# Scores and maxima of a causal attention as float32r products in row halves, the other products cut in row halves, and the causal mask added by a product

## The reference

```python
x = x + 0.5 * ffn(layernorm(x))
x = x + attention(layernorm(x))
x = x + 0.5 * ffn(layernorm(x))

# ffn: x_prev is x shifted by one row
r = sigmoid((mu_r * x + (1 - mu_r) * x_prev) @ W_r.T)
k = (mu_k * x + (1 - mu_k) * x_prev) @ W_k.T
out = r * (square(relu(k)) @ W_v.T)

# attention, per head, after a rotation of q and k by position
att = softmax(where(causal, q @ k.T / sqrt(16), -1e9))
out = (att @ v) @ W_proj + b_proj
```

## Time and profile before

| | us |
|---|---|
| median of 3 runs | 3111.19 |
| lowest and highest | 3110.26, 3119.8 |
| the profiled execution | 3112.07 |
| its span in the trace | 3110.3 |
| TensorE busy | 2962.3 (95%) |
| VectorE busy | 2475.0 (80%) |
| ScalarE busy | 2159.2 (69%) |
| GpSimd busy | 1566.6 (50%) |

### The profile page before, as it was taken

One profiled execution on the slowest core, in us unless ns is written; L12 is line 12 of the kernel. 1 busy time (PEld: TensorE's weight loads), 2 busy tenths in 40 slices (PEclk: granted clock), 3 DMA queues, 4 the chain that ended last, 5 costly groups with the idle time before them and its releaser, 6 DMA issues.

```text
span 3110.3 us, 56224 instructions
## 1 busy us (share of the span) xinstructions
PE 2962.3 (95%) x18245; PEld 1665.9 (54%) x18245; DVE 2475.0 (80%) x7302; ACT 2159.2 (69%) x4802; POOL 1566.6 (50%) x2190
## 2 busy tenths in 40 slices
PE   6899999999999999999999999999999999999997
PEld 4444555555555555555555555555555555555444
DVE  3888888888888888888888887888888888887872
ACT  4477777777777777777777777777767777777664
POOL 5455555555455455555555455454555555454323
PEclk9899999999999999999999999999999999999999
DMA  3443343343434352342443333343442532433421
GB/s 99 79 84 65 64 100 66 83 90 72 86 77 88 69 97 67 76 99 60 91 87 68 88 77 84 80 85 76 79 93 59 98 81 67 93 76 71 83 60 39
DMA packets 202585, 245.49 MB, mean 79 GB/s; under 512 B 68405, under 2 KB 104245, under 8 KB 202293
## 3 DMA queue, kind: packets, MB, share of 16 engines
q1 hardware_dynamic: 202293, 241.90, 37.5%
HBM read 53.48 MB, written 51.38 MB: 34 GB/s over the span
## 4 chain that ended last, share of the span: by engine, by line
PE 66%; DVE 12%; ACT 8%; POOL 6%; issue 6%; DMA 1%; SPq 1%; POOLq 0%; DVEq 0%; ACTq 0%
PE ps_y L735 14%; PE ps_s L704 12%; PE ps_m L714 11%; PE ps_d L794 7%; PE ps_d L788 6%; PE ps_d L791 5%; PE ps_d L800 5%; ACT pt_sb L830 4%; DVE ps_m L943 3%; PE ps_d L781 3%; PE ps_d L742 2%; DVE mx_sb L946 2%; PE ps_d L804 2%; POOL pt_sb L1075 2%; DVE dif_sb L974 2%
## 5 line engine op out<-in xcount | busy, mean ns | idle before, releaser
L830 ACT ACTIVATE pt_sb<-ps_s 128x512 f32<-128x512 f32 (+1 forms) x3039 | 1451.6, 495 | 816.9 <-PE ps_s L704 806.7
L943 DVE CUSTOM_DVE_ANT_0 ps_m<-ps_m,mask_sb 128x128 f32<-128x128 f32 (+3 forms) x2048 | 990.3, 498 | 370.7 <-PE ps_m L714 355.9
L704 PE MATMUL ps_s<-qr_sb,kr_sb 99*128 99x512 bf16 (+1 forms) x3039 | 994.5, 329 | 50.4 <-ACT pt_sb L830 39.3
L714 PE MATMUL ps_m<-kr_sb,qr_sb 96*128 96x512 bf16 (+3 forms) x3072 | 1000.1, 329 | 37.9 <-DVE mx_sb L943 27.7
L946 DVE TENSOR_REDUCE mx_sb<-ps_m 128x1 f32<-128x512 f32 x1024 | 697.9, 682 | 105.7 <-PE ps_m L714 97.3
L1075 POOL TENSOR_SCALAR_AFFINE_SELECT pt_sb<-pt_sb 128x512 f32<-128x512 f32 x512 | 331.4, 647 | 833.8 <-ACT pt_sb L830 833.3
L735 PE MATMUL ps_y<-pt_sb,v_sb 128*32 128x512 f32 (+3 forms) x6144 | 589.9, 494 | 3.6 <-POOL pt_sb L1075 2.7
L704 PEld LDWEIGHTS ps_s<-qr_sb,kr_sb 99*128 99x128 bf16 x3039 | 291.8, 96 | 510.0 <-issue 229.7
L714 PEld LDWEIGHTS ps_m<-kr_sb,qr_sb 96*128 96x128 bf16 x3072 | 302.0, 98 | 319.2 <-DVE mx_sb L943 71.1
L800 PE MATMUL ps_d<-axn_sb,wqk_sb 128*128 128x256 f32 x1024 | 305.3, 396 | 3.9 <-ACT axn_sb L872 3.9
L735 PEld LDWEIGHTS ps_y<-pt_sb,v_sb 128*32 128x32 f32 x6144 | 154.6, 109 | 285.9 <-issue 258.3
(11 more groups left out here) (96 smaller groups left out, 3465.5 us busy)
## 6 DMA issues: line engine op xcount, KB each, us to landing
kr_sb<-part_sb SPq DMA_DIRECT2D x378, 128.0 KB, 4.4
qr_sb<-part_sb SPq DMA_DIRECT2D x378, 128.0 KB, 4.7
y_way<-yt_sb SPq DMA_DIRECT2D x128, 256.0 KB, 2.7
sw_sb<-qb_sb SPq DMA_DIRECT2D x496, 64.0 KB, 2.0
x_sb<-x SPq DMA_DIRECT2D x64, 256.0 KB, 2.8
yn_sb<-y_way SPq DMA_DIRECT2D x64, 256.0 KB
den_sb<-r_way SPq DMA_DIRECT2D x64, 256.0 KB
out<-x_sb SPq DMA_DIRECT2D x64, 256.0 KB, 2.2
```

Of the source, the lines that this page charges most:

```text
L704: eng.matmul(score_bank(slot)[:, 0:width], kr_sb[0:KR + NP, n % RS, j, kb * P:(kb + 1) * P], qr_sb[0:KR + NP, n % RS, j, q0:q0 + width], s ...
L714: eng.matmul(ps_m[:, u % NM, 0:width], qr_sb[0:KR, n % RS, j, i * P:(i + 1) * P], kr_sb[0:KR, n % RS, j, piece * QC:piece * QC + width], s ...
L830: eng.activation(pt_sb[:, buffer, j, column:column + width], score_bank(slot)[:, 0:width], ACT.Exp, scale=SCALE).then_inc(exped, 1)
L943: eng.tensor_tensor_reduce(ps_m[:, u % NM, 0:width], ps_m[:, u % NM, 0:width], mask_sb[:, m0:m0 + width], 1.0, -3e38, ALU.add, ALU.max, be ...
```

## The change

- Scores and maxima become float32r products. q and k are cut into two parts, three pairs of parts make 48 rows (`KR`), and two rows take the maximum. Two of a group's four heads lie in rows 0 to 63 of `qr_sb` and `kr_sb`, two in rows 64 to 127. In each slot the score is in one half of the rows and the maximum in the other. Products less than 256 columns wide are widened to 256.
- The mask is added to a diagonal maximum by a second, bfloat16 product of 128 columns into the same bank (`later_sb`, `pairs_sb`), and VectorE takes all maxima with the plain reduction. There are two banks `ps_m` in place of three, and three `ps_d` in place of two.
- Each planned product is made in two passes over half the rows, "lanes": first with rows 0 to 63, later with rows 64 to 127 added into the same bank. A slot holds one matmul of each lane, lane 1 of one product and lane 0 of the next (`place_pe`). Outside slots -53 to 3071 they stay whole. Transposes are halved too, lane 0 ahead of the score and lane 1 behind the maximum.
- `r_rest` and `r_mid` are gone, and the buffers `qb_sb` and `sw_sb`: the bias goes straight into `part_sb`, so `r_b0` and not `r_hi` now waits for the DMAs that read the batch before. `rows` has three steps of four DMAs in place of six of two. `m_fin` makes two parts; its maxima end 17 slots ahead (`LEAD`). The maxima keep the order of alternating widths (row block 7, 0, 6, 1, ...), now all four heads of one piece in a row.

```diff
-TERMS_Q = (0, 0, 0, 1, 1, 2)
-TERMS_K = (0, 1, 2, 0, 1, 0)
+TERMS_Q = (0, 0, 1)
+TERMS_K = (0, 1, 0)
...
-NP = 3
+NP = 2
+HALF = P // 2
 VW = HS + 1
 VPAD = 32 - VW
-NEG = -1e30
+BIG, TINY = 2.0 ** 55, 2.0 ** -16
 SCALE = HS ** -0.5
 
-NS, NM, ND = 2, 3, 2
+NS, NM, ND = 2, 2, 3
...
-MAX_ORDER = [i for k in range(TT // 2) for i in (TT - 1 - k, k)]
-UNITS = [(i, j, piece) for i in MAX_ORDER for j in range(G) for piece in range(i // KQ + 1)]
-NU = len(UNITS)
-LEAD = 13
+PIECES = [(i, piece) for k in range(TT // 2) for i in (TT - 1 - k, k) for piece in range(i // KQ + 1)]
+LEAD = 17
+NU = GSLOTS
+UNITS = [(PIECES[u // G][0], (u - LEAD) % G ^ 1, PIECES[u // G][1]) for u in range(NU)]
...
+PATIENCE = 3
...
-                    s("ACT", "r_b0", i, 0.36, t, ("r_QK", i, 1), ("r_low", i - 2 if i >= NCH + 2 else -1, 1))
+                    s("ACT", "r_b0", i, 0.36, t, ("r_QK", i, 1), (f"rows{NT - 1}", NG * (b - 1) + 2 * pair + 1, 7))
...
-                    s("ACT", "r_hi", i, 0.53, t, ("r_add", i, 3), (f"rows{NT - 1}", NG * (b - 1) + 2 * pair + 1, 7))
-                    s("POOL", "r_rest", i, 1.2, t, ("r_hi", i, 2))
-                    s("ACT", "r_mid", i, 0.53, t, ("r_rest", i, 3))
-                    s("POOL", "r_low", i, 1.2, t, ("r_mid", i, 2))
+                    s("ACT", "r_hi", i, 0.53, t, ("r_add", i, 3))
+                    s("POOL", "r_low", i, 1.2, t, ("r_hi", i, 2))
...
+    def place_pe(self, chains, slot, mine):
+
+        whole = slot < HALF_MAX or slot >= self.nb * BSLOTS
...
+        if free and self.entire is None and self.lanes[0] is None and not (whole and self.lanes[1]):
+            key = self.pick("PE", chains, slot, None)
+            if key:
+                self.hold(key, free[0])
+                self.slots[key[0] + "+", key[1]] = slot
+                if whole:
+                    self.entire = key, 0
+                else:
+                    self.lanes[0], self.idle = (key, 0), 0
+                    self.divide(key)
...
+        if self.lanes[0] is None and (self.lanes[1] is None or self.idle < PATIENCE and not whole):
+            self.idle += 1
+            return 0, 0
+        done = 0
+        for lane in (1, 0):
+            if self.lanes[lane]:
+                key, u = self.lanes[lane]
+                units = self.steps[key][1]
+                if u < units:
+                    mine.append((*key, u, lane))
+                self.lanes[lane] = key, u + 1
+                if lane == 1 and u + 1 == units:
+                    self.lanes[1] = None
+                    self.slots[key] = slot
+                    done = 1
+                if lane == 0 and u + 1 >= units and self.lanes[1] is None:
+                    self.lanes = [None, (key, 0)]
...
-        part_sb = sb("part_sb", [P, NP, 2, 2, T], BF16)
-        v_sb = sb("v_sb", [P, 2, TT, H * VW + VPAD])
-        qr_sb = sb("qr_sb", [P, RS, G, T], BF16)
-        kr_sb = sb("kr_sb", [P, RS, G, T], BF16)
+        part_sb = sb("part_sb", [P, NP, 2, 2, T])
+        v_sb = sb("v_sb", [P, 2, VPAD + TT * H * VW])
+        qr_sb = sb("qr_sb", [P, RS, G // 2, T], F32R)
+        kr_sb = sb("kr_sb", [P, RS, G // 2, T], F32R)
...
+                            for h in range(2):
+                                r = HALF * h + t * HS
+                                eng.dma_start(dst[r:r + HS, ring, :, cols].bitcast(F32),
+                                              part_sb[base + h:base + 64:2, part, m, n, cols]).then_inc(rows_in[ring], 16)
...
+                rows, more = slice(HALF * (j % 2), HALF * (j % 2) + KR + NP), max(0, CH - width)
+                eng.matmul(score_bank(slot)[:, 0:width + more], kr_sb[rows, n % RS, j // 2, kb * P:(kb + 1) * P],
+                           qr_sb[rows, n % RS, j // 2, q0 - more:q0 + width], start=True, stop=True).then_inc(scored, 1)
...
+                rows, wide = slice(HALF * (j % 2), HALF * (j % 2) + KR), max(CH, width)
+                product = eng.matmul(ps_m[:, u % NM, 0:wide], qr_sb[rows, n % RS, j // 2, i * P:(i + 1) * P],
+                                     kr_sb[rows, n % RS, j // 2, piece * QC:piece * QC + wide], start=True, stop=not diagonal)
+                if diagonal:
+                    half = slice(HALF * (j % 2), HALF * (j % 2) + HALF)
+                    pe.wait_ge(masks_in, 32)
+                    product = eng.matmul(ps_m[:, u % NM, width - P:width], later_sb[half, :], pairs_sb[half, :], start=False, stop=True)
+                product.then_inc(max_made, 1)
...
-            def dense(name, i, u):
+            def dense(name, i, u, lane):
+
                 d = plan.bank[name, i]
-                if u == 0:
+                if u == 0 and not lane:
                     pe.wait_ge(taken[d], plan.nth[name, i])
+                if u == 0 and lane == 1:
+                    pe.wait_ge(half_made[d], plan.split[name, i])
                 ps = ps_d[:, d, :]
                 h, cc = divmod(u, CC)
-                cols, rows = slice(h * P, (h + 1) * P), halves(h)
+                cols, out_cols = slice(h * P, (h + 1) * P), halves(h)
+                k = slice(0, P) if lane is None else slice(HALF * lane, HALF * lane + HALF)
...
+                if u == units - 1:
+                    mm.then_inc(half_made[d] if lane == 0 else made[d], 1)
...
-                m0 = QC + P - width
-                dve.wait_ge(set_pool, N_SET_POOL)
                 dve.wait_ge(max_made, u + 1)
-                best = mx_sb[:, n % 2, piece, j * TT + i:j * TT + i + 1]
-                if diagonal:
-                    eng.tensor_tensor_reduce(ps_m[:, u % NM, 0:width], ps_m[:, u % NM, 0:width], mask_sb[:, m0:m0 + width],
-                                             1.0, -3e38, ALU.add, ALU.max, best).then_inc(max_taken, 1)
-                else:
-                    eng.tensor_reduce(best, ps_m[:, u % NM, 0:width], mybir.AxisListType.X, ALU.max).then_inc(max_taken, 1)
+                m = j % 2 * NH + j // 2 * TT + i
+                eng.tensor_reduce(mx_sb[:, n % 2, piece, m:m + 1], ps_m[:, u % NM, 0:width], mybir.AxisListType.X,
+                                  ALU.max).then_inc(max_taken, 1)
...
-                elif name == "r_rest":
+                elif name == "r_low":
                     pool.wait_ge(r_high, i + 1)
-                    eng.tensor_tensor(biased_of(i), biased_of(i), parts_of(i, 0), ALU.subtract).then_inc(r_rest, 1)
-                elif name == "r_low":
-                    pool.wait_ge(r_mid, i + 1)
-                    eng.tensor_tensor(parts_of(i, 2), biased_of(i), parts_of(i, 1), ALU.subtract).then_inc(r_low, 1)
+                    eng.tensor_tensor(rounded(parts_of(i, 1)), biased_of(i), parts_of(i, 0), ALU.subtract).then_inc(r_low, 1)
```

428 lines of the change are left out of this document (208 added, 220 removed).

## The result

The changed kernel takes 3464.72 us (median of 4, 3460.28 to 3469.01) beside 3113.94 us for the kernel before on the same chip: a ratio of 1.1124, 95% interval 1.11 to 1.1149. It is 11% slower, and slower than the whole range of the forecast. Its profiled execution has a span of 3462.0 us, against 3110.3.

A forecast was written before the change was run, and what follows sets the result against it. TensorE was taken as the bound, 175.7 us of a 187.5 us batch; it falls to 152.1, other engines and waits make it 162 + 13 = 175.0, 12.5 fewer a batch; 3112.1 - 192 = 2920 us, range 2830 to 2990.

The forecast's parts named there:

- TensorE is the bound before, with short waits on banks: Kernel before: TensorE needs 175.7 of a batch's 187.5 us, and 11.8 are left as waits.
- Halves side by side, and float32r at the pace of bfloat16: Assumptions for TensorE: both row halves run at once; scores and maxima fall from 63.6 to 33.4 us a batch.
- in line: Rival: planned passes start strictly in list order, costing 17.2 us a batch; 3020 us in all; chance 0.13.
- slow float32r: Rival: float32r scores and maxima stream at a float32 pass's pace, 0.43 us for 512 columns; 3222 us; chance 0.08.
- not together: Rival: the array's row halves don't run together, so their times add up; 4258 us; chance 0.07.
- 0.22 for a pass of 512: TensorE price of a score or maximum of 512 columns, 0.22 us, read from starts in the kernel before.
- Lane 1's wait is hidden: Lane 1's wait for lane 0's result hides behind the next score and maximum; otherwise 7 us a batch.
- Unevenness 2.8: TensorE's lanes between bursts: a lone lane or uneven halves add 2.8 us a batch.
- VectorE takes back 9.9, ScalarE 2.6, and 13 of waits: Batch summed by stretches between bursts: the two engines take back gain, giving 162.0; 13 more waits give 175.0 us.
- 8 us less around the batches: Outside the batches: 4 us less in the preparation's chain and 4 less in the last 197 us.
- ScalarE's waits grow as much as VectorE's: Sign that would show the forecast wrong; it expected VectorE to be waited for more than ScalarE.
- Waits take all of it: Rival: waits grow from 11.8 to 35 us a batch, no gain left; about 3105, 3060 to 3160; chance 0.08.

The follow-up runs named there:

- b_nm2: The kernel before with two banks for maxima and three for planned products in place of three and two: 3292.11 us, ratio 1.0565.
- bf16pace: Changed kernel, scores and maxima reading only the upper bfloat16 half of each float32r number: 3365.40 us, ratio 1.0804.
- lane01: Changed kernel with lane 0's pass issued ahead of lane 1's within each slot: 3431.56 us, ratio 1.1024.
- m2d3p: Changed kernel, same banks, planner allowed 1.2 planned products a slot (was 1.0) and up to 4 saved up (was 1.5): 3976.17 us, ratio 1.2756.
- lightboth: Changed kernel, VectorE reducing only the last 128 columns of each maximum and ScalarE exponentiating 128 columns of each score: 3131.39 us, ratio 1.0066.
- filler: Changed kernel with 42 extra products of 256 columns a batch ahead of maxima in slots 44 to 71 and 136 to 149: 3436.55 us, ratio 1.1042.
- explight: Changed kernel with ScalarE exponentiating only 128 columns of each score, VectorE's maxima whole: 3399.55 us, ratio 1.0911.
- whole: Changed kernel with all planned products and transposes whole (128 rows), scores and maxima still in row halves: 4047.26 us, ratio 1.3.

## Why the prediction was wrong

By its steps:

- *TensorE is the bound before, with short waits on banks*: right as a ledger, but not the whole of it. By b_nm2 the third bank of maxima is what keeps these waits short, up to 10.9 us a batch.
- *Halves side by side, and float32r at the pace of bfloat16*: right. The rivals "in line", "slow float32r" and "not together" fall with the rows at 1499.83 and 1501.93. The Trainium skill's rule that matmuls start and end strictly in program order ("TensorE: Matmul & The Clock Gate", "The mechanism") does not hold in this trace between row halves: of two passes in different halves, the later in the list started 0.12 us earlier.
- *0.22 for a pass of 512*: short by 0.11 wherever the load stands in front, 5.6 a batch by bf16pace and 12.3 by the count of the lanes. The loads had no term in the sum. The price was taken from products whose loads were done ahead.
- *Masks 3.8*: 3.7 measured. *TensorE 152.1 a batch*: its 142.6 of columns are 137.6.
- *Lane 1's wait is hidden*: nearly; lane01 has 2.0 of the 7 that it could have cost.
- *Unevenness 2.8*: between bursts, for the lanes alone. In m2d3p the spread of the same products over the slots was worth 32 us, the lower clock that came with it included.
- ***VectorE takes back 9.9, ScalarE 2.6, and 13 of waits***: the step that failed. (Its parts don't quite add: 152.1, 9.9 and 2.6 are 164.6, and the sum has 162.0. The 22.9 above is 175.0 less 152.1.) It put the time in which TensorE's lanes stand still at 32.4, with the edges of bursts; the trace has 44.5 of gaps, and 12.3 of loads that stand in front of passes. It took the longest engine over a stretch of some seven slots, which lets an engine that is idle in one slot make it up in another. That needs banks for as many slots as the stretch has; there are two. That the banks matter is shown by b_nm2 (10.9), and that the readers' pace does by lightboth (20.6, the clock's part included). That it acts slot by slot in the changed kernel is argued, from the wait at 1504.20 and from the sum that follows. I have redone the sum with the same durations, pass by pass: a score waits for the exponential two slots back, a maximum for the second maximum before it, and all that stands behind in the list waits too. It gives 181.2 a batch for the kernel before and 179.0 for the changed one, 181.9 with 0.11 for each load that stood behind a wait: next to no gain, where the sum by stretches gave 176.0 and 162.0. For two banks on the kernel before it gives 186.9, half of the loss that was measured. It still misses 23 of 204.8, and has the sign of lane01 wrong, so it is a better sum and no proof; other fair choices of the durations move it by 3 or 4 us.
- *The clock* was not in the prediction at all: 29 us a batch at 1.2 GHz, worth 3.3 at least by filler and 10.4 by the count of the lanes.
- *8 us less around the batches*: there were 99.6 more up to the fourth batch and 78.5 more behind the thirteenth, where three batches at 17.4 would be 52. The first batch took 270.5 us after 209.7, with TensorE at 1.2 GHz and 19.3 of 20 us busy at its start, where the kernel before had 0.92 of the clock. How the 61 us split was not tried.
- *What would show me wrong*: "ScalarE's waits grow as much as VectorE's" did not come: in the list they fell, from 12.8 to 6.4. That ScalarE stands on the path as well shows only in explight and lightboth. VectorE is busy 71% of the middle batch, not over 75%. "Waits take all of it" was the right rival, but 3060 to 3160 stopped where the gain was gone; nothing stops waits there.

In sum, the change took 31 us of columns out of a batch (169.0 by the prediction's counts, 137.6 now), and where 18 us stood beside them, gaps, loads and lower clock are now 67.

## What to carry to other kernels

Before work is taken off the busiest engine, count how many slots its output banks let it run ahead, and make the sum slot by slot with those banks, not over longer stretches: an engine that is idle a third of the time was still on the path here. Splitting the array into row halves asks for more banks, because two products are open at once, and a bank taken from a reader that is busy 80% of the time is dear: 5.65% of the run in b_nm2. The Trainium skill has the warning ("TensorEngine Tiling (Array Packing)", "PSUM Bottleneck"): tiling speeds up TensorE and not the reading of its results; here the rows agree: cutting the readers' work alone gave 20.6 us a batch.

## What I had not expected of the hardware

- With half-height passes TensorE can be 95% and more busy by the profile and be granted 1.2 GHz (0.50 from 1450 to 1470 us, 10.00 and 9.55 of 10 us busy); 84 more passes of 256 columns a batch kept it at 2.4.
- A semaphore wait of a pass in one half holds the passes of the other half that stand behind it (both at 1504.20), although without a wait they pass each other freely.
- Going from half passes to a whole product and back costs about 0.3 us (whole): 0.10 before it, 0.11 for a weight load that no longer runs ahead, 0.09 behind it.
- A float32r product of 512 columns costs 0.23 when it stands behind a running pass, as in bfloat16, and 0.34 with its load in front.
